# Expert outputs accumulated into the output rows by indirect transfers, with all ten shared tiles ahead of the expert blocks

## The reference, cut to what matters

```python
x = x + _L1_ffn_ref(_layernorm(x, axis=-1)[None], ...)[0]
# _L1_ffn_ref, xf = the 1250 normalised rows:
h = xf @ shared_w1 + shared_b1                      # 512 -> 768
z = swiglu5(h, ...) @ shared_w2 + shared_b2         # 384 -> 512
w, idx = top_k(softmax(xf @ gate_w + gate_b), 2); w = w / sum(w)
cw = sum(one_hot(idx, 16) * w[..., None], axis=1)
he = einsum('nd,edh->enh', xf, expert_w1) + expert_b1
oe = einsum('enh,ehd->end', swiglu5(he, ...), expert_w2) + expert_b2
y = einsum('ne,end->nd', cw, oe)
return y + z
```

## Time and profile before

| | |
|---|---|
| device time, median of 3 runs | 1041.78 us (1039.56 to 1045.72) |
| profiled execution, device time | 1040.06 us |
| profiled execution, span of the core | 1038.2 us |
| mean granted TensorE clock | 0.945 of full speed |
| PE busy | 862.6 us (83% of the span) |
| DVE / ACT / POOL busy | 567.2 / 286.6 / 133.9 us |
| HBM read / written | 101.97 / 16.92 MB |

### The profile page before, as it was taken

How to read it: one execution, slowest core, us unless ns; L and a number is a source line. 1 busy time by engine, 2 the same in 40 slices (tenths; PEclk the granted TensorE clock), 3 DMA queues, 4 the chain that set the end, 5 groups by cost and what they waited for, 6 DMA issues and landing times.

```text
span 1038.2 us, 13726 instructions
## 1 busy us (share of the span) xinstructions
PE 862.6 (83%) x3474; PEld 591.2 (57%) x3475; DVE 567.2 (55%) x1389; ACT 286.6 (28%) x582; POOL 133.9 (13%) x192
## 2 busy tenths in 40 slices
PE   1666657999999996887899877998899999999891
PEld 0444444788888884556788754544454554555440
DVE  7999977624225148789124685933333433444263
ACT  1777753115124110434221212011111211221110
POOL 4343330000000030000000001001101110110081
PEclk9999997999999998797999969899999999999995
DMA  5710000000000001000000211062947195413163
GB/s 142 238 59 0 0 1 0 1 1 1 1 1 1 1 26 42 1 1 1 32 10 3 81 51 74 1 233 57 338 172 273 51 341 194 167 51 135 43 172 125
DMA packets 38642, 80.91 MB, mean 78 GB/s; under 512 B 7304, under 2 KB 7554, under 8 KB 38602
## 3 DMA queue, kind: packets, MB, share of 16 engines
q1 hardware_dynamic: 27850, 60.55, 17.0%
q0 software_dynamic: 6720, 12.49, 4.1%
q10 hardware_dynamic: 4032, 7.34, 1.9%
HBM read 101.97 MB, written 16.92 MB: 115 GB/s over the span
## 4 chain that ended last, share of the span: by engine, by line
PE 63%; DVE 17%; issue 7%; DMA 4%; ACT 3%; POOL 2%; DVEq 1%; SPq 0%; ACTq 0%; POOLq 0%
PE PS L902 18%; PE PS L1117 13%; PE PS L932 8%; PE PS L1150 7%; PE PS L1025 4%; DVE ET L1311 4%; DMA WB<-in_b 3%; DVE ET L1309 3%; PE PS L971 3%; PE PS L1105 3%; PE PS L1135 2%; ACT YF L768 1%; POOL GB L577 1%; POOL GA L577 1%; DMA GB<-y_dram,slot_i 1%
## 5 line engine op out<-in xcount | busy, mean ns | idle before, releaser
L902 PE MATMUL PS<-CTR,YH 125*128 125x500 f32 (+1 forms) x480 | 167.0, 363 | 3.9 <-DVE YL L1397 3.4
L902 PE MATMUL PS<-CTR,YL 125*128 125x500 f32 (+1 forms) x480 | 165.1, 359 | 0.0
L1117 PE MATMUL PS<-WB,YF 128*128 x448 | 150.2, 489 | 7.3 <-DMA WB<-in_b 5.0
L1117 PEld LDWEIGHTS PS<-WB,YF 128*128 128x128 f32 x448 | 84.0, 190 | 76.0 <-issue 23.9
L843 PE MATMUL PS<-ET 125*125 125x240 f16 x330 | 81.6, 413 | 46.4 <-issue 32.9
L902 PEld LDWEIGHTS PS<-CTR,YH 125*128 125x128 f32 x480 | 92.1, 192 | 22.5 <-DVE YL L1397 9.9
L1311 DVE TENSOR_SCALAR ET<-ET 125x240 f16<-125x240 f16 x330 | 104.1, 347 | 0.0
L902 PEld LDWEIGHTS PS<-CTR,YL 125*128 125x128 f32 x480 | 92.6, 193 | 12.6
L843 PEld LDWEIGHTS PS<-ET 125*125 125x125 f16 x330 | 58.6, 220 | 69.1 <-issue 34.2
L1150 PE MATMUL PS<-WB,YF 128*128 x168 | 79.4, 609 | 12.2 <-ACT YF L768 11.0
L768 ACT COPY YF<-PS 128x384 f32<-128x384 f32 (+1 forms) x38 | 18.2, 478 | 212.7 <-PE PS L1127 212.7
(11 more groups left out here) (319 smaller groups left out, 1332.1 us busy)
## 6 DMA issues: line engine op xcount, KB each, us to landing
WB<-in_w SPq DMA_DIRECT2D x28, 1536.0 KB
WB<-in_w SPq DMA_DIRECT2D x28, 768.0 KB
WB<-in_b SPq DMA_DIRECT2D x28, 384.0 KB
y_dram<-YF ACTq DMA_DIRECT2D x28, 256.0 KB
y_dram<-XTF SPq DMA_DIRECT2D x1, 4352.0 KB, 14.0
X<-in_x SPq DMA_DIRECT2D x1, 2500.0 KB
xn_dram<-XN SPq DMA_DIRECT2D x1, 2500.0 KB
out<-X SPq DMA_DIRECT2D x10, 250.0 KB
```

The costliest lines, as they stand in the source:

```text
L902: mm = nc.tensor.matmul(dest, lhs, rhs, start=(t == 0 and h == 0), stop=(t == NT - 1 and h == 1))
L1117: mm = nc.tensor.matmul(PS[:, 2 * k + h, 0:INTER], xgt[:, k, f, :], WB[:, bass.ds(off + (f * H2 + h * INTER), INTER)], start=(f == 0), sto ...
```

## The change

1. `EARLY = NT`: all ten shared tiles run ahead of the experts; their loops at the ends of PE, DVE and ACT are gone.
2. SP stores `X` to `out` as soon as all shared tiles are added, between its third and its fourth weight load.
3. `y_dram`, `store`, the 20 transfers back, the sums `GA + GB` and `X + GA` are gone. Instead POOL's `scatter(b)` adds `yo[b % 2]` to the rows of `out` by an indirect transfer with `compute_op=ALU.add`. Their row numbers are in `home`, made from `tok`; padding slots go to 128 spare rows behind the output. It waits until scatter b-1 has landed (`scattered`), for `out_stored`, and for `yo_ready` of block b.
4. In POOL's program gather(b) is followed by scatter(b-2) (`AHEAD = 2`). ACT's `result(b)` waits until scatter b-2 has landed.

```diff
-EARLY = 6
+EARLY = NT
+AHEAD = 2
...
-            for b in range(4):
+            for b in range(NWB):
+                load_weights(b // 2, b % 2, b)
+            for t in range(NT):
+                sp.wait_ge(z_added, t + 1)
+                sp.dma_start(out[t * NP:(t + 1) * NP, :], X[0:NP, t, :]).then_inc(out_stored, 16)
+            for b in range(NWB, 4):
                 load_weights(b // 2, b % 2, b)
...
+            def scatter(k, b):
+                if isinstance(b, int):
+                    turn, seen = b + 1, 16 * b
+                else:
+                    turn, seen = pool.to_reg(b + 1), pool.to_reg(b * 16)
+                if not (isinstance(b, int) and b < 1):
+                    pool.wait_ge(scattered, seen)
+                pool.tensor_copy(dest_i[:, k:k + 1], home[:, bass.ds(b, 1)]).then_inc(dest_ready, 1)
+                pool.wait_ge(out_stored, 16 * NT)
+                pool.wait_ge(yo_ready, turn)
+                pool.wait_ge(dest_ready, turn)
+                pool.indirect_dma_start(out[:, :], bass.IndirectOffsetOnAxis(dest_i[:, k:k + 1], 0), yo[:, k, :], None,
+                                        compute_op=ALU.add).then_inc(scattered, 16)
...
-            for b in range(2):
-                gather(0, b, b)
+            for b in range(AHEAD):
+                gather(0, b % 2, b)
+            pool.wait_ge(zeroed, 16)
             last = last_pair(pool)
-            with pool.Fori(1, NB // 2) as i:
+            for b in range(AHEAD, AHEAD + 2):
+                gather(0, b % 2, b)
+                scatter(b % 2, b - AHEAD)
+            with pool.Fori(AHEAD // 2 + 1, NB // 2) as i:
                 with pool.If(i < last + 1):
                     for k in range(2):
                         gather(i, k, i * 2 + k)
...
-            for t in range(NT):
-                for k, dest in enumerate((GA, GB)):
-                    pool.indirect_dma_start(dest[0:NP, t, :], None, y_dram[:, :],
-                                            bass.IndirectOffsetOnAxis(slot_i[0:NP, k, t:t + 1], 0)
-                                            ).then_inc(back_in[t // 2], 16)
...
+                        scatter(k, i * 2 + (k - AHEAD))
+            for j in range(AHEAD):
+                scatter(j % 2, last * 2 + (j + 2 - AHEAD))
+            pool.wait_ge(scattered, pool.to_reg(last * 32 + 32))
...
-            def store(i, k, b):
-
-                act.wait_ge(yo_ready, b + 1)
-                act.dma_start(y_dram[bass.ds(b * BS, BS), :], yo[:, k, :]).then_inc(stored[k], 16)
-
             def result(i, k, b, first=False):
                 act.wait_ge(y_done, b + (EARLY + 1))
                 if not first:
-                    act.wait_ge(stored[k], i * 16)
+                    act.wait_ge(scattered, act.to_reg(b * 16 - 16))
...
             v.tensor_copy(tok[:, :], PS[:, 4, 0:NB])
-            v.tensor_copy(wslot[:, :], PS[:, 4, NB:2 * NB]).then_inc(tables_ready, 1)
+            link(v.tensor_copy(wslot[:, :], PS[:, 4, NB:2 * NB]))
+            link(v.tensor_scalar(padrow, nodef[:, 0:1], float(N), None, ALU.add))
+            link(v.tensor_scalar(filled, wslot[:, :], 0.0, None, ALU.not_equal))
+            link(v.scalar_tensor_tensor(out=filled, in0=PS[:, 4, 0:NB], scalar=padrow, in1=filled,
+                                        op0=ALU.subtract, op1=ALU.mult))
+            v.tensor_scalar(home, filled, padrow, None, ALU.add).then_inc(tables_ready, 1)
...
-    out = nc.dram_tensor("out", (N, D), F32, kind="ExternalOutput").ap()
+    out = nc.dram_tensor("out", (N + BS, D), F32, kind="ExternalOutput").ap()
```

More of the change, by code:

```diff
@@ L154, in build @@
         assert R_ZL + NWB * WBUF * 4 <= R_SW and 2 * ROWB <= NWB * WBUF * 4
-        GA, GB = [at(n, r, [128, NT, D]) for n, r in (("GA", R_ZL), ("GB", R_ZL + ROWB))]
         used = [0]
@@ L251, in build @@
         tt_ps, tt_ready, y_done, yo_ready = sem("tt_ps"), sem("tt_ready"), sem("y_done"), sem("yo_ready")
-        stored = [sem("stored0"), sem("stored1")]
+        dest_ready, scattered = sem("dest_ready"), sem("scattered")
         zeroed = sem("zeroed")
@@ L255, in build @@
         cw_ps, cwt_ready = sem("cw_ps"), sem("cwt_ready")
-        back_in = [sem(f"back_in{g}") for g in range(NT // 2)]
-        sum_ready, out_stored = sem("sum_ready"), sem("out_stored")
+        out_stored = sem("out_stored")
         xn_dram = nc.dram_tensor("xn_dram", [N, D], F32, kind="Internal")
-        y_dram = nc.dram_tensor("y_dram", [NB * BS, D], F32, kind="Internal")
         w1f = FFNR[0:FK3, 0:W1C]
@@ L335, in build @@
         idx = sb("idx", [128, 2], I32)
+        dest_i = sb("dest_i", [128, 2], I32)
+        padrow, filled = rcarve(1), rcarve(NB)
+        home = rcarve(NB).bitcast(I32)
         idx_ready = sem("idx_ready")
@@ L394, in _ @@
             sp.wait_ge(const_done, 5)
-            sp.dma_start(y_dram[SURE * BS:NB * BS, :].rearrange("(b p) d -> p b d", p=BS),
-                         XT[:, 0:D].rearrange("p (o d) -> p o d", o=1).to_broadcast([128, NB - SURE, D])
-                         ).then_inc(zeroed, 16)
+            sp.dma_start(out[N:N + BS, :], XT[:, 0:D]).then_inc(zeroed, 16)
             sp.wait_ge(agg_ready, FT * len(SPLITS) * LAYERS)
@@ L450, in _ @@
                         load_weights(i, k, i * 2 + k)
-            for t in range(NT):
-                sp.wait_ge(sum_ready, t + 1)
-                sp.dma_start(out[t * NP:(t + 1) * NP, :], X[0:NP, t, :]).then_inc(out_stored, 16)
+            sp.wait_ge(zeroed, 16)
             sp.wait_ge(out_stored, 16 * NT)
@@ L569, in _ @@
                         gather(i, k, i * 2 + k)
[L571 to L575, removed]
-                for k, dest in enumerate((GA, GB)):
-                    pool.indirect_dma_start(dest[0:NP, t, :], None, y_dram[:, :],
-                                            bass.IndirectOffsetOnAxis(slot_i[0:NP, k, t:t + 1], 0)
-                                            ).then_inc(back_in[t // 2], 16)
-            for g in range(NT // 2):
-                pool.wait_ge(back_in[g], 16 * 4)
+                        scatter(k, i * 2 + (k - AHEAD))
+            for j in range(AHEAD):
+                scatter(j % 2, last * 2 + (j + 2 - AHEAD))
+            pool.wait_ge(scattered, pool.to_reg(last * 32 + 32))
         @block.scalar
@@ L807, in _ @@
                 with act.If(i < last + 1):
-                    store(i, 0, i * 2 - 2)
                     turn_t(1, i * 2 + (EARLY - 1))
@@ L815, in _ @@
                         result(i - 1, 1, i * 2 - 1)
-                    store(i, 1, i * 2 - 1)
                     turn_t(0, i * 2 + EARLY)
@@ L819, in _ @@
                     result(i, 0, i * 2)
-            store(0, 0, last * 2)
             turn_t(1, last * 2 + (EARLY + 1))
-            sigmoid(0, last * 2 + (EARLY + 2))
             result(last, 1, last * 2 + 1)
[L824 to L828, removed]
         @block.tensor
@@ L1177, in _ @@
                 shared_up(p % 2, p, p)
-                if p == EARLY - 3:
+                if p == 3:
                     pe.wait_ge(slots_ready, 1)
@@ L1217, in _ @@
                     down(i, 0, i * 2)
-            shared_up(0, last * 2 + (EARLY + 2), EARLY)
             turn_act(1, last * 2 + (EARLY + 1))
             down(last, 1, last * 2 + 1)
[L1222 to L1230, removed]
         @block.vector
@@ L1789, in _ @@
             v.tensor_copy(tok[:, :], PS[:, 4, 0:NB])
-            v.tensor_copy(wslot[:, :], PS[:, 4, NB:2 * NB]).then_inc(tables_ready, 1)
+            link(v.tensor_copy(wslot[:, :], PS[:, 4, NB:2 * NB]))
[4 more added lines that the diff above has]
+            v.tensor_scalar(home, filled, padrow, None, ALU.add).then_inc(tables_ready, 1)
             dve.wait_ge(tables_ready, 1)
             last = last_pair(dve)
[L1793 to L1798, removed]
+            for p in range(4, EARLY):
+                z_add(p - 2, p - 2)
+                units(p % 2, p)
             rows_copy(0, 0)
@@ L1813, in _ @@
                     units(1, i * 2 + (EARLY + 1), i * 2 + 1, next_rows)
[L1815 to L1836, removed]
 def kernel(**inputs):
@@ L1881 @@
            for k, v in arrays.items()}
-    out = nc.dram_tensor("out", (N, D), F32, kind="ExternalOutput").ap()
+    out = nc.dram_tensor("out", (N + BS, D), F32, kind="ExternalOutput").ap()
     build(nc, aps, out)
     r = run_bass_kernel_spmd(nc, [{"in_" + k: v for k, v in arrays.items()}], core_ids=[0])
-    return r.results[0]["out"]
+    return r.results[0]["out"][0:N]
```

## The result

The changed kernel takes 1186.22 us (median of 4 runs, 1184.40 to 1186.86), the kernel before 1041.88 us beside it: a ratio of 1.139, 95% interval 1.136 to 1.141. The forecast was 1113, its range ended at 1165, and the highest sum among its bounds was 1183. The profiled execution took 1186.86 us; its span is 1185.2.

A forecast was written before the change was run, and what follows sets the result against it. Blocks, bound by PE's instruction stream before, would be bound by a closed result-scatter-gather chain. Result 0 at 764.2, +312 chain, +14 low clock, +13.7 last results, then final scatters: end 1111.7, forecast 1113 us; range 1068 to 1165.

The forecast's parts named there:

- the chain of one block: Block loop: result b-1, scatter b-1, gather b+2, turning b+2, down b, result b; 11.3 us quiet, 13.8 beside a load.
- PE's clock: Turn and down run 3.4 us longer at the low clock after idling; 4 of 12 loaded blocks, +14 us.
- the gather's landing beside a load: Landing of a gather issued in the middle of a weight load: 5.9 us, in 12 of 25 blocks; 3.4 when quiet.
- result 0 ends: Start of the blocks: four shared tiles moved ahead, 40.8 us, put the end of result 0 at 764.2.
- result to gather's issue, x25: POOL's part of each block: scatter's release, dispatch and issue, then the gather's copy and dispatch, 3.28 us.
- gather's issue to turning, x25: Each block: gather's landing, 3.4 us quiet or 5.9 beside a load, then hand-over to PE of about 0.15.
- turning to result, with the clock, x25: PE and ACT in each block: 4.44 us from turning to the result's end, plus 14 us in all for low clock.
- results 26 and 27: End of the block stage: the last two results after result 25 add 13.7 us, reaching 1103.9.
- last scatter's issue, landing and end: After result 27: scatter 27 issued at 1106.3, 5 us landing to 1111.3, end 0.4 later at 1111.7.
- low clock in nearly every loaded block: Rival on PE in the block loop: 12 x 3.4 = 41 us instead of 14, 1140 us; chance 0.15.
- the rival of a slow accumulation: Block loop: scatter landing of 11.0 us with the gather stuck behind it, 17.4 us a block, 1239 us; chance 0.12.
- The prize: Whole kernel without any new wait: tail's transfers, sums and late stores gone, span end 1023.7, 14.5 us less than 1038.2.

The follow-up runs named there:

- the kernel without loads: The changed kernel with no expert weights loaded from block 4 on, blocks computing with old weights: 1144.30 us, 1.095 of the kernel before.
- the filler: The changed kernel with four unread matmuls ahead of PE's wait for each gather from block 3 on: 1164.53 us, 1.116 of the kernel before.
- the kernel with the gather ahead: The changed kernel with gather b just ahead of scatter b-3 in POOL's program instead of just behind it: 1037.43 us, 0.994 of the kernel before.

## Why the forecast was right in kind and too small

The mechanism was right at each link: 25 waits of PE for gathers, the scatter's wait for the result, the chain of one block, and 12 long circles. The step that failed is the size of two terms, above all **PE's clock**: +14 us in the forecast, some +48 by the traces. The second is the gather's landing beside a load. The sum by the forecast's own steps, predicted and measured:

| term | predicted | measured | miss |
|---|---|---|---|
| result 0 ends | 764.2 | 768.66 | +4.5 |
| result to gather's issue, x25 | 82.0 | 84.2 | +2.2 |
| gather's issue to turning, x25 | 118.8 | 138.6 | +19.8 |
| turning to result, with the clock, x25 | 111 + 14 | 165.8 | +40.8 |
| results 26 and 27 | 13.7 | 17.3 | +3.6 |
| last scatter's issue, landing and end | 7.8 | 10.7 | +2.9 |

The first column adds up to 1111.5, near the forecast's 1111.7, the second to 1185.3, the span (1185.2) but for rounding. The forecast's last step is off by 2 us in itself: with the two offsets that it names, 1.9 and 1.7, 1111.7 gives 1115.3 and not 1113. And its stated range ended at 1165 although its own upper sum was 1183, with long landings and the low clock in all 12 loaded blocks.

**The clock.** "I let 4 of the 12 loaded blocks meet it: +14 us." It was 22 of all 25, and the step took 55 us more than 25 times 4.44. The three circles at full clock took 4.69 each, so 6 of the 55 us have nothing to do with the clock and 48 do, 2.2 a circle where I had 3.4: the price of one was too high and the count far too low. Of the kernel before I had read the step from one block, its shortest; in the other 24 it took 4.75 to 4.77. For the clock I had one row of it falling, after 4.73 us, and took shorter idles to be free; no row of before showed an idle of 2 to 3 us coming back every 12 us. That only loaded blocks would suffer is refuted by the kernel without loads (164.8 us) and by the filler, which brings the quiet blocks back to 4.4. The rival "low clock in nearly every loaded block" (1140, chance 0.15) was nearest and still too narrow. By the kernels, of 78.5 us that the circles lose when loads and low clock are both taken away, the loads alone are 40.7, the filler alone 23.0, and 15 need both, since each leaves the other's idling behind.

**The landing.** I took 5.9 beside a load from one gather and kept 7.5 for the upper bound. The gather now goes out 3.9 us into a load and behind a scatter, and from its issue to the turning it is 7.5 us on average in the loaded circles, 3.7 in the others: the row that I set aside as special was the one that fitted. With plain scatters it is shorter by 0.5 us a circle.

**The issue.** The scatter takes 1.60 us on POOL, not 1.2, and the copy behind it 0.78, not 0.18, but it starts before the issue ends: 3.37 us against 3.28.

**The accumulation.** Its landing was 4.5 to 4.9 us undisturbed, my 5, but 8.2 to 9.4 beside loads. Even so it is off the chain, since every scatter waited last for its result (28 waits for ACT): in the loaded circle shown above it frees POOL at 875.60, 6.7 us before the next result starts. So the rival of a slow accumulation is out, and no gather landed later than 8.0 us. The Trainium skill ("DMA: Bandwidth & Descriptors", Anatomy of one DMA) gives by its formula an estimate of 2.6 us for 256 KB. The plain scatters' 2.7 to 3.0 us without a load beside them agree; the gathers' 3.3 at the least and the accumulating scatters' 4.5 don't.

**Start and end.** Block 0's up took 7.12 us at a clock of 0.76 with only 0.93 us of idling ahead of it; the kernel with the gather ahead had result 0 at 764.22, exactly the forecast, and the first scatter starts at 765.1 to 769.5 in the kernels with the same start: a spread for which I had no term and have no cause. The end's +6.5 us are ACT's empty rounds with the low clock behind them (+3.6) and the 5 us behind the last landing, where I took 0.4, less 1.7 us since the last scatter was issued sooner behind its result.

**The prize.** Without the new wait I expected a span of 1023.7; the kernel with the gather ahead has 1035.0. Its 11.3 us are accounted for: 4.2 in the blocks (one of 15.6 us, where up waits 3.53 us for its bias and then runs 8.05 us at the low clock), 4.4 in the last two results, 4.6 behind the landing, less 1.9 us because the last scatter followed its result sooner than forecast. What was argued and not tried: that block of 15.6 us comes from scatters and loads sharing the DMA engines.

## What to carry to other kernels

A prefetch and a consumer-side transfer in one in-order queue must be read in queue order: whatever the transfer waits for, the prefetch behind it waits for too, and one place earlier or later can be the whole result (149 us here). When a chain leaves the matmul engine idle once a block, cost the slower clock in every block, short idles included, until a row shows otherwise. And when several rows give a latency, take the one whose neighbours (what is queued ahead, what else moves) match the new place, even if it is the extreme.

## What the runs showed of the hardware

- In the changed kernel the granted clock fell in 22 of 25 blocks, after idles of 2.25 to 6.8 us that came back every 12 to 19 us; in three with 1.95, 2.06 and 2.25 us it held. With plain scatters it also fell after idles of 1.49 to 2.00 us, in 7 of 13 blocks. Without weight loads it held once after 2.73 us. The length of one idle alone does not tell these cases apart. Unread matmuls in the idle time made the whole kernel 22 us faster.
- An accumulating indirect transfer of 128 rows of 2 KB took 1.57 to 1.64 us to issue and 4.5 to 4.9 us to land, 8.2 to 9.4 beside a weight load; a plain one 0.99 to 1.02, and 2.7 to 3.0 or 6.7 to 8.4.
- A copy on POOL right behind a scatter's issue shows 0.78 us instead of 0.18.
- The span ended 5 us after the last landing where POOL waited for it, 2.6 us in the one profile where ACT did.
